# Layer 1 of a two-layer decoder: a new written order for TensorE's steps

## The reference, cut to what matters

```python
# Mamba-2 block, per sequence (8 heads of 64, state 128)
z, xBC, dt = split(x @ in_proj_w.T)
xBC = silu(causal_conv(xBC, 4 taps)); dt = softplus(dt + dt_bias)
y = scan(exp(-dt*exp(A_log)), x*dt, B, C) + D*x
y = y * silu(z)
y = y * rsqrt(mean(y*y) + 1e-5) * norm_w        # the squares
x = layernorm(x + y @ out_proj_w.T)
# mLSTM block reading the context (4 heads of 64)
ig, fg = [x, c, c] @ gate_kernels + bias        # the gates
C = (q k^T / 8) * exp(cumulated log-forget gates, stabilised by their maximum)
h = C/(max(|sum C|, exp(-max)) + 1e-6) @ v;  x = layernorm(x + headnorm(h)*scale)
# feed-forward with binarised weights
bw = mean(|w|) * sign(w);  x = layernorm(x + gelu(x @ bw1.T + b1) @ bw2.T + b2)
```

## Time and profile before

| what | value |
|---|---|
| median of three executions | 1183.35 us (1179.50 to 1188.39) |
| profiled execution | 1180.75 us, span 1178.9 us |
| TensorE busy, whole span | 1122.6 us (95%) |
| VectorE, ScalarE, GpSimd busy | 827.5, 688.1, 324.6 us |
| mean granted TensorE clock, whole span | 0.972 |

### The profile page before, as it was taken

How to read it: one execution, slowest core, us unless ns; L and a number is a source line. 1 busy time by engine, 2 the same in 40 slices (tenths; PEclk the granted TensorE clock), 3 DMA queues, 4 the chain that set the end, 5 groups by cost and what they waited for, 6 DMA issues and landing times.

```text
span 1178.9 us, 23661 instructions
## 1 busy us (share of the span) xinstructions
PE 1122.6 (95%) x8692; PEld 933.1 (79%) x8692; DVE 827.5 (70%) x2589; ACT 688.1 (58%) x1435; POOL 324.6 (28%) x354
## 2 busy tenths in 40 slices
...
GB/s 330 109 19 1 2 1 1 55 19 2 1 1 1 55 19 2 2 1 2 37 19 75 2 46 46 72 1 1 1 28 1 28 27 11 1 28 37 19 10 18
...
## 3 DMA queue, kind: packets, MB, share of 16 engines
...
## 4 chain that ended last, share of the span: by engine, by line
PE 77%; DVE 12%; ACT 7%; issue 2%; POOL 0%; DMA 0%; DVEq 0%; SPq 0%; ACTq 0%
PE ps L498 47%; PE ps L654 4%; PE ps L672 2%; PE ps L671 2%; PE ps L646 2%; DVE z L1631 2%; PE ps L644 2%; PE ps L670 2%; DVE arena L1831 2%; PE ps L914 1%; PE ps L610 1%; PE ps L701 1%; PE ps L513 1%; DVE pq L1475 1%; ACT arena L1392 1%
## 5 line engine op out<-in xcount | busy, mean ns | idle before, releaser
L498 PE MATMUL ps<-wts,arena 128*128 128x256 f32 (+2 forms) x1008 | 197.7, 352 | 5.2 <-ACT arena L1392 3.2
L2150 POOL TENSOR_TENSOR pq<-pq 128x512 f16<-128x512 f32 x72 | 83.9, 1166 | 405.4 <-ACT pq L1239 405.4
L498 PE MATMUL ps<-arena,wts 128*128 128x256 f16 (+1 forms) x1344 | 184.0, 289 | 8.8 <-DVE arena L1445 6.5
L498 PEld LDWEIGHTS ps<-wts,arena 128*128 128x128 f32 (+1 forms) x1008 | 151.4, 152 | 40.9 <-ACT arena L1392 4.0
L498 PEld LDWEIGHTS ps<-arena,wts 128*128 128x128 f16 (+1 forms) x1344 | 149.1, 112 | 30.5 <-DVE arena L1445 6.9
L1631 DVE SCALAR_TENSOR_TENSOR z<-ps,small,z 128x256 f32<-128x256 f32 x256 | 123.9, 484 | 22.9 <-PE ps L498 6.0
L1516 DVE CUSTOM_DVE_ANT_0 pq<-ps,mb 128x128 f32<-128x128 f32 x128 | 36.8, 288 | 105.9 <-PE ps L646 105.3
L498 PE MATMUL ps<-wts,pq 128*128 128x256 f16 x864 | 106.4, 273 | 4.5 <-DVE z L1631 1.7
L498 PEld LDWEIGHTS ps<-wts,pq 128*128 128x128 f16 x864 | 83.4, 98 | 17.8 <-POOL pq L2150 3.4
L1236 ACT ACTIVATE pq<-ps 128x512 f32<-128x512 f32 x72 | 42.8, 595 | 83.8 <-PE ps L498 83.3
L1097 ACT ACTIVATE lnv<-mv,eps 128x2 f32<-128x2 f32 (+1 forms) x48 | 14.3, 298 | 131.6 <-DVE mv L1423 131.5
...
## 6 DMA issues: line engine op xcount, KB each, us to landing
...
```

The source lines that it names most:

```text
L498: ins = mm(out_, l, r, start=(n == 0), stop=(n == len(pairs) - 1))
L2150: G.tensor_tensor(lo, abuf(s, e), hi, ALU.subtract).then_inc(*po.up(("alo", s, e)))
```

## The change

`PE_ORDER` has the same 317 steps in another order. `ACT_ORDER` is only broken into lines differently: word by word it is the same. Nothing else changes. 181 of the 317 steps have another place in the list, most by one or two places; the furthest moves are `0.zg.0.2` and `0.zg.0.0` (7 places earlier), `0.up.0.0` (5 earlier), and 4 earlier or later for some of `in`, `tr`, `decay` and `2.rms.0`. The order of takes gives some steps other banks, and two swaps (`0.cell.0.1` with `1.decay.0.3`, `3.decay.1.2` with `3.decay.1.3`) give those four other buffers. The places of the list around the gates and the squares, from the diff:

```diff
@@ turn 0's gates.1, turn 1's rms.0
-    0.read.0.0 0.cell.0.1 1.decay.0.3 1.in.1.2 0.score.0.1 1.zg.1.0 0.ztb.1 0.read.0.1 1.scan.0.3 0.gates.1
-    1.rms.0 1.xs.1 2.dt.0 1.zg.1.2 2.load.1 1.cb.1 1.out.0 2.in.0.2 2.in.0.4 1.decay.1.2 2.dsum.0 2.dt.1
+    0.read.0.0 1.decay.0.3 0.cell.0.1 1.in.1.2 0.score.0.1 1.zg.1.0 0.ztb.1 0.read.0.1 1.scan.0.3 0.gates.1
+    1.zg.1.2 1.rms.0 1.xs.1 2.dt.0 2.load.1 1.out.0 1.cb.1 2.in.0.2 2.dsum.0 1.decay.1.2 2.in.0.4 2.zg.0.0
@@ 1.gates.0, 1.rms.1
-    2.zg.0.0 2.in.0.0 1.decay.1.0 2.zg.0.2 1.ztb.0 2.csrow.0 1.scan.1.2 1.decay.1.3 1.gates.0 1.scan.1.0
-    0.gain.1 2.cb.0 0.rows.1 1.scan.1.3 0.ztc.0 1.decay.1.1 3.load.0 0.cols.1 0.cell.1.1 0.up.0.6 3.dt.0
-    1.scan.1.1 1.gain.0 2.dsum.1 0.score.1.1 2.csrow.1 1.rms.1 0.read.1.1 0.cell.1.0 0.score.1.0 0.up.0.0
+    2.in.0.0 2.dt.1 1.ztb.0 1.decay.1.0 2.csrow.0 1.scan.1.2 2.zg.0.2 1.gates.0 1.scan.1.0 0.gain.1 1.decay.1.3
+    2.cb.0 0.rows.1 1.scan.1.3 0.ztc.0 1.decay.1.1 3.load.0 0.up.0.6 0.cols.1 0.cell.1.1 3.dt.0 1.scan.1.1
+    1.gain.0 0.score.1.1 2.dsum.1 0.up.0.0 2.csrow.1 1.rms.1 0.cell.1.0 0.read.1.1 0.score.1.0 1.rows.0 2.xs.0
@@ 1.gates.1, 2.rms.0
-    2.in.1.4 2.zg.1.2 1.cell.0.0 1.score.0.0 2.scan.0.0 0.down.0 1.ztb.1 1.read.0.0 0.ztc.1 1.gates.1 2.scan.0.2
-    2.scan.0.3 1.read.0.1 2.zg.1.0 2.scan.0.1 1.cols.1 3.dsum.0 1.cell.1.1 0.down.1 2.rms.0 1.score.1.1 2.xs.1
-    2.out.0 2.decay.1.0 1.read.1.1 2.decay.1.2 2.decay.1.3 2.scan.1.0 2.ztb.0 3.in.0.0 2.decay.1.1 3.in.0.2
+    2.in.1.4 2.in.1.2 1.score.0.0 2.zg.1.2 0.down.0 0.ztc.1 1.ztb.1 1.read.0.0 2.scan.0.2 1.gates.1 2.in.1.0
+    1.read.0.1 1.cols.1 2.zg.1.0 2.scan.0.1 1.cell.1.1 3.dsum.0 0.down.1 1.score.1.1 2.out.0 1.read.1.1 2.xs.1
+    2.rms.0 2.decay.1.0 3.in.0.0 2.decay.1.2 3.in.0.2 2.decay.1.3 2.decay.1.1 2.scan.1.0 2.ztb.0 2.scan.1.2
@@ turn 2: gates.0, rms.1, gates.1
-    1.ztc.0 2.scan.1.2 2.scan.1.3 1.cell.1.0 3.csrow.0 1.up.0.2 3.in.0.4 1.score.1.0 1.up.0.0 2.gates.0 1.up.0.4
-    2.gain.0 3.decay.0.3 2.rows.0 3.scan.0.2 2.rms.1 3.decay.0.1 3.in.1.0 2.cols.0 3.in.1.4 2.cell.0.0
-    3.scan.0.3 3.decay.1.2 3.decay.1.3 1.down.0 2.gates.1 2.cell.0.1 3.scan.1.2 2.score.0.1 1.ztc.1 3.scan.0.1
+    2.scan.1.3 1.ztc.0 3.csrow.0 3.in.0.4 1.cell.1.0 1.up.0.0 1.up.0.2 2.gates.0 1.score.1.0 1.up.0.4 2.scan.1.1
+    3.decay.0.3 2.rows.0 3.in.1.0 3.scan.0.2 3.decay.0.1 2.rms.1 2.cols.0 3.in.1.4 2.cell.0.0 3.zg.1.2 3.dsum.1
+    3.decay.1.2 1.down.0 2.cell.0.1 2.gates.1 3.scan.1.2 1.ztc.1 2.score.0.1 3.scan.0.1 3.scan.1.3 3.decay.1.0
@@ turn 3: rms.0, gates.0, rms.1, gates.1
-    3.scan.1.3 3.decay.1.0 3.decay.1.1 1.up.1.0 2.gain.1 2.read.0.1 2.rows.1 3.rms.0 1.up.1.2 2.cols.1
-    2.cell.1.1 3.out.0 2.score.1.1 3.scan.1.0 2.cell.1.0 1.up.1.6 2.score.1.0 2.read.1.1 3.ztb.0 3.scan.1.1
-    1.up.1.4 3.gates.0 2.read.1.0 2.ztc.0 1.down.1 2.up.0.0 3.gain.0 3.rms.1 3.rows.0 2.up.0.4 2.up.0.6 3.cols.0
-    3.cell.0.0 3.score.0.0 2.up.0.2 3.out.1 3.cell.0.1 2.down.0 3.read.0.0 3.ztb.1 3.score.0.1 2.ztc.1 3.gates.1
+    3.decay.1.1 2.read.0.1 2.gain.1 1.up.1.0 2.rows.1 3.rms.0 3.out.0 2.cols.1 1.up.1.2 2.cell.1.1 2.score.1.1
+    3.scan.1.0 1.up.1.6 2.cell.1.0 2.score.1.0 3.ztb.0 2.read.1.1 3.scan.1.1 3.gates.0 1.up.1.4 2.ztc.0
+    2.read.1.0 1.down.1 2.up.0.0 3.gain.0 3.rows.0 3.rms.1 2.up.0.4 2.up.0.6 3.cols.0 3.cell.0.0 2.up.0.2
+    3.out.1 3.score.0.0 3.cell.0.1 2.down.0 3.read.0.0 3.ztb.1 2.ztc.1 3.score.0.1 3.gates.1 3.read.0.1 2.up.1.0
```

And the beginning of the list, where `al2` waits for VectorE:

```diff
-    0.load.0 0.load.1 0.in.0.2 0.in.0.0 0.zg.1.2 0.dt.0 -.al2 -.tr.0.1.4 0.zg.0.2 -.tr.1.0.0 -.tr.1.1.0 0.in.1.4
+    0.load.0 0.zg.0.2 0.load.1 0.dt.0 0.in.0.2 0.in.0.0 -.tr.0.1.4 -.al2 0.zg.1.2 -.tr.1.0.0 -.tr.1.5.0
```

75 lines of the change are left out of this document (39 added, 36 removed).

## The result

The changed kernel took 1194.37 us (median of seven executions, 1192.76 to 1200.95); the kernel before took 1181.72 us beside it (seven, 1179.46 to 1188.39). The ratio is 1.0111, 95% interval 1.0076 to 1.0147. Forecast were 1177 us, 1167 to 1188. The profiled execution of after took 1193.04 us, 12.3 more than the one of before.

The account below looks back on a forecast made before the run. TensorE, busy for 95% of the span, was taken as the bound, with layer 1's clock the larger item; -10.6 (falls spared) + 2.7 (new falls) + 1.5 (waits) = -6.4 us gave 1177 us, range 1167 to 1188.

Parts of the forecast that it names:

- Moves that touch waits: Waits from moved steps: 1.5 us lost at `2.rms.0` (bounds 0 and 6.6), 0 at the start and for other moves.
- The other moves are of one to four places: Small moves across the list, within the drains' order on ScalarE and VectorE: 0 within 1.5 us either way.
- the start: Moves of `0.zg` and `tr` steps around the 4.40 us wait for `al2`: 0, bounds -0.5 and +1 us.
- What a stretch costs: Half-clock stretches: wide work loses half, narrow about a third; eight last 40.6 us, so at most 20.3 us to win.
- The eight places: Half-clock stretches at or right behind `gates` or `rms` steps in layer 1: new neighbours win 10.6 us in all.
- Against it: `2.gates.0`, `2.gates.1`, `2.rms.0`, `2.rms.1`, without a fall before, fall in four of ten cases: 2.7 us lost, bounds 0 and 6.8.
- under 30: Sign for the forecast: under 30 us of half clock between 855 and 1125, in place of 40.6.
- the 37 named as wrong: Sign against the forecast: the half-clock total is 37 us or more.
- the 0.94 named: Sign for the forecast: a clock of layer 1 at 0.94 or more.
- Falls only move: Rival, chance 0.22: as many clock falls come at other places; 1180 to 1187 us.
- the forecast 0.55: Main case, chance 0.55: four to six of the eight half-clock stretches shrink or go; 1171 to 1180 us.
- the rival that put 1190 to 1195 on it: Rival, chance 0.08: ScalarE's queue stands at `2.rms.0`, TensorE idles near 980 to 990 and a fall follows.

Follow-up runs that it names:

- experiment 1: The kernel before with the products of gates and squares put out as 128 columns in place of 8 and 1: 1168.93 us, ratio 0.9873.
- experiment 2: The changed kernel (new order) with the products of gates and squares put out as 128 columns: 1183.34 us, ratio 1.0000 to the kernel before.
- experiment 5: The kernel of experiment 2 with the lists of ScalarE and VectorE made to follow TensorE's new order: 1190.55 us, ratio 1.0067 to the kernel before.
- Experiments 6 and 10: The kernel of experiment 1 with the new TensorE order only in steps 67 to 160 (1174.47 us), or only in steps 180 to 205 (1171.47 us).
- experiment 9: The kernel of experiment 1 with the new TensorE order only in steps 104 to 118: 1172.86 us, ratio 0.9922 to the kernel before.
- experiment 12: The kernel of experiment 2 with three steps put back behind work of their own block: 1188.94 us, ratio 1.0035 to the kernel before.
- experiment 8: The kernel before with the products of the gates alone put out as 128 columns, the squares left narrow: 1182.26 us, ratio 0.9992.

## Why the prediction was wrong

**The step that failed** is "Moves that touch waits", and in it the sentence "The other moves are of one to four places ...: 0 within 1.5 either way". They cost some 12 of the 14 us of waits that came (the start brought 2.1); with wide products in both orders it is 16 us of waits (experiments 1 and 2). I had priced one large move (`2.rms.0`) and the start, and had taken the small ones as free because each is small. Nearly all of the 181 moved steps are such moves, in a list in which VectorE and ScalarE run without a gap for stretches of 5 us and more; fourteen more steps than before wait for over 0.25 us (37 against 23), mostly 0.5 to 2 us each. Nor do the moves stay "within the drains' own order": the pairs that ScalarE drains in another order than TensorE's went from 29 to 69, though experiment 5 shows that to mend this is not enough. Experiments 6 and 10 show that they arise where the order changed, experiment 9 that some need the new order ahead as well, experiment 12 that three of them can't be mended singly. The bound was badly taken too: "the whole of other waits" says nothing of waits that a new order makes.

Of the 18.8 us between the -6.4 of the sum and the +12.4 of the profiled executions, these waits are 12.6 (14.1 in place of 1.5), the clock is 5.5 (2.4 won in place of 7.9), the start of the layer 0.7.

**What a stretch costs** was right for TensorE's own work, but not as what the kernel gains. Experiment 1 takes 30 us of half clock away and the clock's part falls by 15.5 us, half of it. But the waits come up by 7 (35.1 to 42), since the other engines do not become faster (VectorE is busy for 322 us of layer 1 in both): the profiled execution is 8.5 us shorter, the median 13.3. From after to experiment 2 it is 23.4 of clock against 9 of waits. So some of the 16 us of waits between experiments 1 and 2 may be due to the better clock of the second. Two readings were off besides, without a part in the sum. Narrow work does not lose "about a third" of a stretch: the fall began 1.0 us into the 2.70 us, and 1.0 + 1.7 / 2 is about the 1.84 of full clock, so it loses half too. And 252 and 257 ns are not "hardly less than a wide one": the 256-column float32 instructions of the same line have 387 and 400 ns.

**The eight places.** Forecast 10.6 won, 2.7 lost. Measured, the stretches at narrow steps add up to 51.1 us (in the list of after, all but the first and the last) against 40.6: at half of it 5.2 lost, where 7.9 were to be won. That the clock's part shrank by 2.4 all the same comes from the falls behind waits, which the forecast had left out: 10.2 and 6.7 us in the earlier trace rows and 6.8 at `al2`, in after 3.4 (756.1) and 3.4 (1172.5). The one at `al2`, in the kernel before:

```profile
753.70:760.50 6.80, 5.34 (x17) 4.52 (x18) 6.45 (x17) 5.52 (x7) 0.00 (x0) 0.50 0.44 131
```

- Right: `1.rms.0`, a fall of 3.4 at 865.3 in place of 10.2; `3.rms.0`, `1.rms.1` and `3.rms.1` without a fall; `1.gates.1` and its 3.4 unchanged.
- Wrong: `1.gates.0` keeps its 6.8; `3.gates.0` doubled to 6.8; `3.gates.1` went from 3.4 to 13.7.
- "Against it": `2.gates.0` fell for 6.8 and `2.rms.1` for 3.4, `2.rms.0` and `2.gates.1` not. `0.gates.0` and `0.rms.1` fell too, 3.4 each, and had not been named.

Between 855 and 1125 the half clock is 3.4 + 6.8 + 3.4 + 6.8 + 3.4 + 6.8 = 30.6 us, a little over the "under 30" and short of the 37 named as wrong, but `0.gates.0`, `0.rms.1` and nearly all of the 13.7 lie outside that stretch. The clock of layer 1 is 0.93, short of the 0.94 named. The rival **Falls only move** described the clock best: as many narrow steps fall, at other places. I gave it 0.22 and the forecast 0.55, though its arguments against were about the kernel before alone.

**`2.rms.0`** went as written: it starts at 980.94, and ScalarE idled 8.16 us for it. ScalarE's timeline in after (answers to the earlier trace rows):

```profile
982.82 0.26 ACT L1299 ACTIVATE small<-ps,eps 128x2 f32<-128x2 f32 x1 [8.16 <-PE ps L498]
```

TensorE did not idle between 980 and 992: the cover held, the price of 1.5 was too high by that much, and the rival that put 1190 to 1195 on it has the measured 1194.37 in its range by luck, with the wrong mechanism. The start: steps 0 to 27 wait 2.1 us more and save 1.0 of clock, +1.1 in place of 0. `al2` no longer waits 4.40, but `tr.0.1.4` waits 3.24 ahead of it, and `0.in.1.0` and its neighbours more than before.

**The sign of the sum.** "I am wrong if ... TensorE's waits in layer 1 pass 35 us": they are 38.25.

The Trainium skill's rule against the change ("TensorE: Matmul & The Clock Gate", section "Why this matters for your kernels": drops in the middle come from idle gaps) fails for the unwidened kernels: TensorE is busy for all of the 3.40 us at 865.3, with no idle time just ahead, and for all of 13.70 us at the largest fall, with 0.96 us of idle time ahead of it. It agrees with experiment 1, in which the falls that are left all follow waits. The same table of the Trainium skill advises to pad thin matmuls (M under 512), since the clock otherwise swings with every K-tile of the loop. Experiment 1 does not test this: what it pads is the number of moving columns, and M, the 128 rows of the result, stays as it is.

**What stays open.** Which of the many late drains pulls the others along was not settled: experiment 12 shows waits come up further on, not where the chain begins. Nor was it why a wait of 2.3 to 2.4 us has a fall behind it in one execution and none in another. Nor why the same list gives falls of another length from one execution to the next (experiment 8: 1173 or 1182).
